# First attention of a two-layer kernel: the transposed maxima move from the maxima's banks to the scores' banks

## The reference

```
qkv = zn @ w_qkv                      # 16 heads of 8
scores = einsum('bhqd,bhkd->bhqk', q, k) / SCALING
att = softmax(scores, axis=-1)
out = einsum('bhal,bhlv->bhav', att, v)
out = out @ w_proj + b_proj
```

## Time and profile before

| | |
|---|---|
| profiled execution: span | 1372.0 us |
| median of three runs | 1371.8 us |
| TensorE matmul busy | 1249.1 us, 91% |
| VectorE busy | 1009.4 us, 74% |
| ScalarE busy | 851.8 us, 62% |
| GpSimd busy | 237.5 us, 17% |
| first attention, first to last exponential | 116.6 to about 811 us |

### The profile page before, as it was taken

How to read it: one execution, slowest core, us unless ns; L and a number is a source line. 1 busy time by engine, 2 the same in 40 slices (tenths; PEclk the granted TensorE clock), 3 DMA queues, 4 the chain that set the end, 5 groups by cost and what they waited for, 6 DMA issues and landing times. The chain is left out here.

```text
span 1372.0 us, 25967 instructions
## 1 busy us (share of the span) xinstructions
PE 1249.1 (91%) x10305; PEld 580.1 (42%) x10305; DVE 1009.4 (74%) x1288; ACT 851.8 (62%) x1447; POOL 237.5 (17%) x309
## 2 busy tenths in 40 slices
PE   6968999999999999999999978998899899899980
PEld 4631222222222222222222225555699566688870
DVE  6878898998899989998999737665676588623324
ACT  3533888888888888888888866555421366533431
POOL 4200110000000000000000002000385222135560
PEclk9986999999999999999999989998999599999995
DMA  5763033232323313222231121100011111123316
GB/s 147 202 199 79 26 65 64 50 76 45 74 64 82 76 40 78 51 66 66 50 74 40 69 71 48 47 16 16 17 31 39 55 44 36 46 69 102 100 58 188
DMA packets 75204, 94.96 MB, mean 69 GB/s; under 512 B 13236, under 2 KB 44684, under 8 KB 74052
## 3 DMA queue, kind: packets, MB, share of 16 engines
q1 hardware_dynamic: 69996, 83.19, 23.9%
q0 software_dynamic: 5088, 10.12, 2.4%
HBM read 54.30 MB, written 38.56 MB: 68 GB/s over the span
## 5 line engine op out<-in xcount | busy, mean ns | idle before, releaser
L670 ACT ACTIVATE b_exp_ring<-psum 128x512 f32<-128x512 f32 x1024 | 555.6, 600 | 148.8 <-PE psum L725 145.6
L612 DVE TENSOR_REDUCE b_mx<-psum 128x2 f32<-128x1024 f32 x507 | 595.8, 1218 | 66.5 <-PE psum L557 65.4
L725 PE MATMUL psum<-b_q,b_k 75*128 75x512 bf16 x1024 | 312.4, 387 | 1.5 <-ACT b_exp_ring L670 1.5
L701 PE MATMUL psum<-b_exp_ring,b_v 128*32 128x512 f32 x2048 | 274.5, 608 | 0.9 <-ACT b_exp_ring L670 0.7
L725 PEld LDWEIGHTS psum<-b_q,b_k 75*128 75x128 bf16 x1024 | 79.3, 97 | 317.0 <-ACT b_exp_ring L670 221.8
L556 PE MATMUL psum<-b_k,b_q 64*128 64x512 bf16 x512 | 168.9, 395 | 25.5 <-DVE b_mx L612 10.6
L557 PE MATMUL psum<-b_ko,b_qo 64*128 64x512 bf16 x512 | 168.9, 395 | 0.0
L740 POOL CAST b_neg<-b_neg_rest 16x128 bf16<-16x128 f32 x32 | 8.9, 279 | 639.6 <-DVE b_neg_rest L623 639.6
L1834 ACT ACTIVATE e_hT<-psum,e_b 128x358 f32<-128x358 f32 (+3 forms) x96 | 53.6, 559 | 75.4 <-PE psum L1854 72.0
L556 PEld LDWEIGHTS psum<-b_k,b_q 64*128 64x128 bf16 x512 | 44.7, 93 | 128.6 <-DVE b_mx L612 41.4
L701 PEld LDWEIGHTS psum<-b_exp_ring,b_v 128*32 128x32 f32 x2048 | 41.3, 108 | 108.6 <-issue 106.0
(11 more groups left out here) (278 smaller groups left out, 1427.6 us busy)
## 6 DMA issues: line engine op xcount, KB each, us to landing
b_q<-q_ops SPq DMA_DIRECT2D x48, 192.0 KB
b_k<-k_ops SPq DMA_DIRECT2D x48, 192.0 KB
k_ops<-a_k SPq DMA_DIRECT2D x20, 256.0 KB, 3.3
x_disp<-b_zeros SPq DMA_DIRECT2D x13, 320.0 KB
e_x<-x_disp SPq DMA_DIRECT2D x8, 520.0 KB
v_ops<-a_vs SPq DMA_DIRECT2D x4, 1024.0 KB, 5.1
b_v<-v_ops SPq DMA_DIRECT2D x16, 256.0 KB
av_out<-b_acc SPq DMA_DIRECT2D x128, 32.0 KB, 1.7
```

Source lines behind the costliest of these rows:

```text
L612: nc.vector.reduce_max(mx[:, d % 2, :, i // 2, i % 2], pair, AX.X).then_inc(sem("b_max_done"), 1)
L670: act.activation(ex[:, n % E_RING, :], g.bank(5 + n % 3), ACT.Exp, scale=ATT_SCALE)\
L701: last = nc.tensor.matmul(AV[32 * i:32 * i + 32, :], v[s][:, at_v:at_v + 32], ex[:, (4 * group + i) % E_RING, :], start=(kb == 0), stop=(k ...
L725: nc.tensor.matmul(g.bank(5 + n % 3), k[s][0:XROWS, h, kb * P:(kb + 1) * P], q[s][0:XROWS, h, half * BANK:(half + 1) * BANK], start=True, ...
```

## The change

- `max_items` goes; the maxima's sequence holds the 512 items alone, two behind each group, `MAX_LEAD` = 10 past the first item of the duo after.
- The sequence of the score banks gets the transposed maxima as units of their own (`score_units`): `(0, None)` first, and `(d+1, None)` ahead of the tiles of group `T_GROUP` = 4 of duo d. TensorE transposes into the next of banks 5 to 7; ScalarE copies the 16x128 negated to a new tile `b_neg_all`; GpSimd casts the first part, subtracts, casts the second and subtracts again. SyncE stores each part when it is there.
- VectorE folds the halves of duo d (`both_halves`) after the reduction of the first item of duo d+1.
- VectorE's reciprocals stand behind an item number; the multiplication for `d_oT` stands behind the last item.

```diff
-ITEMS = MAXES + 1
-LATE = 2
-T_GROUP = 5
-LEAD = ITEMS + LATE - 2 * T_GROUP
+NMAX = DUOS * MAXES
+MAX_LEAD = 10
+T_GROUP = 4
...
+def score_units():
+
+    seq = [(0, None)]
     for d in range(DUOS):
+        for kb in range(TB):
+            if kb == T_GROUP and d + 1 < DUOS:
+                seq.append((d + 1, None))
+            seq += [(d, 4 * kb + i) for i in range(4)]
+    return seq
...
+    units = score_units()
+    place = {unit: n for n, unit in enumerate(units)}
+    issued = lambda d, kb: min(NMAX, MAXES * (d + 1) + 2 * kb + MAX_LEAD)
...
+            def both_halves(d):
+                dve.wait_ge(sem("b_max_done"), MAXES * (d + 1))
+                nc.vector.reduce_max(m[:, d % 2, :], mx[:, d % 2, :, :, :].rearrange("p h t a -> p (h t) a"),
+                                     AX.X).then_inc(sem("b_m"), 1)
+
+            for n in range(FIRST, NMAX):
                 item(n)
+                if n >= MAXES and n % MAXES == 0:
+                    both_halves(n // MAXES - 1)
+                d = n // MAXES - 1
                 b = d // 8 - 1
+                if 0 <= b < RECS and d % 8 == 3 and n % MAXES == 8:
                     dve.wait_ge(sem("d_dens"), 16 * (b + 1))
                     nc.vector.reciprocal(dens[:, b, :], dens[:, b, :]).then_inc(sem("d_recs"), 1)
+            both_halves(DUOS - 1)
+            for b in range(EARLY):
+                dve.wait_ge(sem("d_loaded"), 32 * (b + 1))
+                nc.vector.tensor_tensor(oT[:, b, :], num[:, :], den[:, :], ALU.mult).then_inc(sem("d_oT"), 1)
...
+            def negated_maxima(d, bank):
+                if d:
+                    act.wait_ge(sem("b_third"), d)
+                act.activation(neg_all[:, :], bank[0:MAXES, 0:P], ACT.Copy, scale=-1.0).then_inc(sem("b_exp_done"), 1)
...
+            def bank_of(n):
+                if n >= 3:
+                    pe.wait_ge(sem("b_exp_done"), n - 2)
+                return g.bank(5 + n % 3)
+
+            def transposed_maxima(d):
+                pe.wait_ge(sem("b_m"), d + 1)
+                to = bank_of(place[d, None])
+                nc.tensor.transpose(to[0:MAXES, 0:P], m[:, d % 2, :], g.ident[:, :]).then_inc(sem("b_scores"), 1)
...
+            for n in range(FIRST, MAXES + 2):
+                item(n)
+            transposed_maxima(0)
+            for n in range(MAXES + 2, issued(0, 0)):
                 item(n)
             for d in range(DUOS):
                 pe.wait_ge(sem("b_m_loaded"), 16 * NPART * (d + 1))
                 for kb in range(TB):
                     if d == DUOS - 1 and kb in PROJECT_AT:
                         project_piece(PROJECT_AT.index(kb))
+                    n = issued(d, kb)
+                    if kb == T_GROUP and d + 1 < DUOS:
+                        transposed_maxima(d + 1)
+                    scores(d, 4 * kb)
+                    scores(d, 4 * kb + 1)
+                    scores(d, 4 * kb + 2)
+                    if d + kb:
+                        times_v(TB * d + kb - 1)
+                    scores(d, 4 * kb + 3)
+                    for i in range(n, min(n + 2, NMAX)):
+                        item(i)
...
             def parts(d):
-                pool.wait_ge(sem("b_max_done"), seq.index((d, None)) + 1)
+                pool.wait_ge(sem("b_exp_done"), place[d, None] + 1)
+                if d:
+                    pool.wait_ge(sem("b_m_loaded"), 16 * NPART * d)
+                nc.gpsimd.tensor_copy(neg[:, 0, :], neg_all[:, :]).then_inc(sem("b_first"), 1)
+                pool.wait_ge(sem("b_first"), d + 1)
+                nc.gpsimd.tensor_tensor(neg_rest[:, :], neg_all[:, :], neg[:, 0, :], ALU.subtract)\
+                  .then_inc(sem("b_rest"), 1)
+                pool.wait_ge(sem("b_rest"), d + 1)
                 nc.gpsimd.tensor_copy(neg[:, 1, :], neg_rest[:, :]).then_inc(sem("b_second"), 1)
...
-                    if i == 0:
-                        sp.wait_ge(sem("b_max_done"), seq.index((d, None)) + 1)
-                    else:
-                        sp.wait_ge(sem(("b_second", "b_third")[i - 1]), d + 1)
+                    sp.wait_ge(sem(("b_first", "b_second", "b_third")[i]), d + 1)
```

More of the change, by code:

```diff
@@ L557, in maxima_scores @@
     return g.nc.tensor.matmul(g.bank(2 * (n % 2) + 1), qo[MROWS:P, p, t], ko[MROWS:P, p, keys], start=True, stop=True)
-def max_items():
-    seq = []
+def score_units():
+    seq = [(0, None)]
     for d in range(DUOS):
[L564 to L568, removed]
+        for kb in range(TB):
[3 more added lines that the diff above has]
+    return seq
 def layer0_attention(g):
@@ L583, in layer0_attention @@
         m = sb("b_m", [P, 2, MAXES])
+        neg_all = sb("b_neg_all", [MAXES, P])
         neg_rest = sb("b_neg_rest", [MAXES, P])
@@ L598, in layer0_attention @@
     AV = g.bank(4)
-    seq = max_items()
-    through = lambda kb: 2 * (kb + 1) + (kb >= T_GROUP)
-    upto = lambda d, kb: min(len(seq), ITEMS * (d + 1) - 1 + LEAD + through(kb))
+    units = score_units()
+    place = {unit: n for n, unit in enumerate(units)}
+    issued = lambda d, kb: min(NMAX, MAXES * (d + 1) + 2 * kb + MAX_LEAD)
     with nc.Block() as block:
@@ L607, in item @@
             def item(n):
-                d, i = seq[n]
+                d, i = n // MAXES, n % MAXES
                 dve.wait_ge(sem("b_max_scores"), n + 1)
[L610 to L626, removed]
+                pair = g.bank(2 * (n % 2), 2).rearrange("p (h x) -> p h x", h=2)
@@ L627, in _ @@
+                nc.vector.reduce_max(mx[:, d % 2, :, i // 2, i % 2], pair, AX.X).then_inc(sem("b_max_done"), 1)
+            def both_halves(d):
[3 more added lines that the diff above has]
+            for n in range(FIRST, NMAX):
                 item(n)
-            for d in range(DUOS):
-                for n in range(upto(d, -1), upto(d, TB - 1)):
-                    item(n)
+                if n >= MAXES and n % MAXES == 0:
+                    both_halves(n // MAXES - 1)
+                d = n // MAXES - 1
@@ L631, in _ @@
                 b = d // 8 - 1
-                if 0 <= b < RECS and d % 8 == 3:
+                if 0 <= b < RECS and d % 8 == 3 and n % MAXES == 8:
                     dve.wait_ge(sem("d_dens"), 16 * (b + 1))
                     nc.vector.reciprocal(dens[:, b, :], dens[:, b, :]).then_inc(sem("d_recs"), 1)
-                if 0 <= b < EARLY and d % 8 == 7:
-                    dve.wait_ge(sem("d_loaded"), 32 * (b + 1))
-                    nc.vector.tensor_tensor(oT[:, b, :], num[:, :], den[:, :], ALU.mult).then_inc(sem("d_oT"), 1)
+            both_halves(DUOS - 1)
@@ L662, in evacuate @@
                 act.activation(acc[:, d % 2, :], AV, ACT.Copy).then_inc(sem("b_acc"), 1)
[L664 to L673, removed]
+            def negated_maxima(d, bank):
+                if d:
+                    act.wait_ge(sem("b_third"), d)
+                act.activation(neg_all[:, :], bank[0:MAXES, 0:P], ACT.Copy, scale=-1.0).then_inc(sem("b_exp_done"), 1)
+            for n, (d, u) in enumerate(units):
+                act.wait_ge(sem("b_scores"), n + 1)
+                if u is None:
+                    negated_maxima(d, g.bank(5 + n % 3))
+                    continue
+                e = 4 * TB * d + u
+                if e >= E_RING:
+                    act.wait_ge(sem("b_av"), (e - E_RING) // 4 + 1)
+                act.activation(ex[:, e % E_RING, :], g.bank(5 + n % 3), ACT.Exp, scale=ATT_SCALE)\
+                   .then_inc(sem("b_exp_done"), 1)
+                if u == 3 and d:
+                    evacuate(d - 1)
             evacuate(DUOS - 1)
@@ L684, in item, with scores @@
                     pe.wait_ge(sem("b_max_done"), n - 1)
[L685 to L689, removed]
-                maxima_scores(g, q[s], k[s], qo[s], ko[s], n, p, i).then_inc(sem("b_max_scores"), 1)
+                maxima_scores(g, q[s], k[s], qo[s], ko[s], n, p, i).then_inc(sem("b_max_scores"), 1)
+            def bank_of(n):
[6 more added lines that the diff above has]
+                nc.tensor.transpose(to[0:MAXES, 0:P], m[:, d % 2, :], g.ident[:, :]).then_inc(sem("b_scores"), 1)
+            def scores(d, u):
+                s, h, kb, half = d // 2 % SLOTS, 2 * (d % 2) + u % 4 // 2, u // 4, u % 2
+                nc.tensor.matmul(bank_of(place[d, u]), k[s][0:XROWS, h, kb * P:(kb + 1) * P],
+                                 q[s][0:XROWS, h, half * BANK:(half + 1) * BANK], start=True, stop=True)\
+                  .then_inc(sem("b_scores"), 1)
             def times_v(group):
@@ L695, in times_v @@
                 s, p = d // 2 % SLOTS, d % 2
-                pe.wait_ge(sem("b_exp_done"), 4 * (group + 1))
+                pe.wait_ge(sem("b_exp_done"), place[d, 4 * kb + 3] + 1)
                 if kb == 0 and d:
@@ L706, in project_piece @@
                 if piece == 0:
-                    pe.wait_ge(sem("b_max_done"), len(seq))
+                    pe.wait_ge(sem("b_max_done"), NMAX)
                     pe.wait_ge(sem("d_oT"), 1)
@@ L712, in _ @@
```

(6 more changed lines are left out.)

## The result

The changed kernel takes 1399.9 us (median of four runs, 1396.0 to 1406.2) against 1371.6 before. The ratio is 1.021, 95% interval 1.018 to 1.025: slower, by 28 us. The forecast was 1401 within 1392 to 1410. The profiled execution is the fastest of the four: span 1394.3 us, against 1372.0 before.

A forecast was written before the change was run, and what follows sets the result against it. It took TensorE (98.3% busy) to bound the middle of the first attention, VectorE close behind. Terms 47.7 - 19.5 + 1.5 - 0.7 - 0.2 = +28.8 us on a span of 1372.0 gave 1400.8, forecast 1401, range 1392 to 1410.

The forecast's parts named there:

- The wait for the fold: Transposition ahead of group 4 waits for VectorE's fold, queued behind a just-issued item's reduction: +1.59 us a duo, +47.7 us.
- What is removed: The longer group with the old transposed maxima goes (3.26 us against 2.61): 0.65 us a duo, -19.5 us over 30 duos.
- the ring: Three score banks: the third score tile behind the transposition waits 0.11 us a duo for ScalarE's copy.
- The net of a duo: Per duo (eight groups of four score tiles): +1.59 us of wait less 0.65 removed; duos of 22.6 us, not 21.64.
- The clock: Rival: each stall in the first attention lowers TensorE's clock, 4 us lost each, 120 in all, 1521 us; chance 0.03.
- The reciprocals: VectorE's three reciprocals in the first attention stay; no cost was counted for them.
- The start: Before the first scores: 26 items instead of 24, +2.26 us, less a 0.79 interruption; together +1.5 us.
- oT: Its multiplication moves behind the last maximum, where VectorE is idle: -0.7 us.
- The last transposition: The stage's last transposition waits less for its fold: -0.2 us, bounds -0.5 and +0.3.
- the chain of parts: GpSimd's parts and their stores: 6.0 us at worst after the transposition, 10.4 available; hidden, 4 us to spare.
- The 0.05 of signalling: Added to the transposition-to-copy time and ScalarE's copy, 0.32 + 0.28 + 0.05 = 0.65 us, before the third score tile starts.
- The rule on TensorE's order: Matmuls stay in program order, so ready scores cannot pass the waiting transposition; otherwise the first rival's 1360 us, chance 0.06.

The follow-up runs named there:

- taken away in two ways: Changed kernel with VectorE's fold ahead of the first item's reduction: 1357.7 us; or changed kernel with the transposed maxima one group later (T_GROUP = 5): 1361.1 us.
- the fold first: Changed kernel with VectorE folding duo d+1's halves ahead of the reduction of duo d+2's first item, not behind it: 1357.7 us, ratio 0.990.
- a lead of 4: Kernel with the fold ahead of the reduction, plus MAX_LEAD = 4, transposed maxima in group 7, reciprocals behind the second item: 1424.8 us, ratio 1.041.

## Why the prediction was right, step by step

The stage by itself, from its first matmul to the end of its last copy out of bank 4, took 718.9 us before (94.36 to 813.29) and 746.3 after (95.17 to 841.50): +27.4. The stages behind took 558.7 and 552.8 in the two profiled executions, although nothing was changed in them; their stretches at the lower clock lie elsewhere (between 1060 and 1100 us at 0.57 to 0.58 before; after, 0.72 and 0.68 between 1080 and 1120), and in the other profiled kernels they took 555.1 to 557.2. This is why the profiled span is 6 us under the forecast while the median is 1 us from it. Single runs lie between 1396.0 and 1406.2 us, so that last agreement, to 1 us, is closer than the terms deserve.

- **The wait for the fold** was the mechanism, at its place and in its size. Forecast 1.91 us from item to transposition, measured 1.81; forecast 4.20 from item to item, measured 4.08; +1.47 a duo in place of +1.59. The term that was off is from the fold's start to the transposition: 0.34 us was read in the one place of the earlier trace rows, and 0.24 it is (313.36 to 313.60; in the changed kernel's last duo 0.25, 809.82 to 810.07). Why the kernel before has 0.1 more there stays open. That the wait is the cause is shown from three sides: taken away in two ways the kernel is 39 to 42 us faster, lengthened by one reduction the duo is 1.12 us longer.
- **What is removed.** A duo without the stall is 21.19 us against 21.64: -0.45. With 0.20 for the transposition and the ring in it, what went is 0.65, as forecast; the seven other groups take 21.19 - 2.81 = 18.38 us, as before (21.64 - 3.26). Nothing came of VectorE's two operations fewer, as assumed.
- **The net of a duo**: 22.46 - 21.64 = +0.82, against 1.59 - 0.65 = 0.94; thirty make +24.6 instead of +28.2.
- **The clock** was no term of the sum, and as a rival (a fall each time, 4 us each) it was wrong both ways: it falls after some of the stalls, 2 and 6 of 30, and a fall costs 1.53 us. +3.1 to +9.2 us. The row before 1196.32 showed that a gap of 1.41 us may leave the clock alone, and I took "may" for "does". By luck this about makes up for the smaller stall, which left the net 3.6 us under the forecast.
- **The reciprocals** were written down as unchanged. They stand now between the two items of a group and not between groups: 0.77 us a duo and not 0.39, three times, +1.1. A step that is moved has to be priced at its new place.
- **The start.** First scores 22.9 us after the stage's first matmul and not 21.6: +1.3, forecast +1.5. But most of it was given back. The clock rose just before 128 us before and just after 126 us in the changed kernel (granted 0.53 and 0.93 in the stretch from 126 to 128), so the later start spent less time at 1.2 GHz: duo 0's result left bank 4 28.6 us after the first scores before, and 27.7 after, with a stall of 0.8 in it.
- **oT** behind the last item: its duo is 22.46 us like the others, -0.7 as forecast.
- **The last transposition** waited 0.37 us for its fold and not 0.48: 0.1 of the 0.2 us forecast is seen.
- **ScalarE and GpSimd**: 0.09 us of ring a duo (forecast 0.11), and the chain of parts hidden. The 0.05 of signalling stood on no row of before; in the changed kernel the copy ends at 314.18 and the weight load of the third score tile, which waited for it, starts at 314.23.

In the stage: 24.6 + 3.1 + 1.1 + 1.3 - 0.7 = 29.4, less about 1.7 for duo 0's shorter slow part (28.6 - 27.7, and the stall of 0.8 in it) is 27.7; measured 27.4, where the forecast had 28.8.

The rule on TensorE's order held: the scores of group 4 never passed the waiting transposition. Of the rule that idle gaps between bursts put the clock back (the Trainium skill, "TensorE: Matmul & The Clock Gate", Why this matters for your kernels) this case shows that gaps shorter than those the page warns of count too: stalls of 1.20 us in dense work did it in 2 and in 6 of 30 cases, stalls of 2.33 us in 9 of 30.

## What to carry to other kernels

Where an in-order engine waits for a small result, read from the consumer's place what was *issued last to the producer* ahead of that result; one reduction too many there, issued just before the wait, cost this kernel 1.2 us thirty times, and moving one line turned 2.1% slower into 1.0% faster. Price an instruction that is moved at its new place even if it is the same instruction. A short stall in an otherwise dense stage can cost more than its length, because the clock may fall after it; look for such falls in the granted clock by stretches and in the length of the single duos, not in the spread of the runs, which doesn't tell here.

The best kernels here, with the fold first, the transposed maxima in group 5 or 6 with a lead of 8 or 6, and the reciprocals between groups, take 1352.6 and 1352.0 us: 1.2 to 1.3% under the kernel before, and 47 us under the changed one. Between these two there is no difference that was measured.

## What was not expected of the hardware

The clock's falls. After stalls of 1.20 us it fell in 2, then in 6 of 30 duos of the same kernel, at other places each time, and cost 1.53 us. After stalls of 2.33 us it fell in 9 of 30 and cost 3.0 to 4.4 us. In the kernel with a lead of 4 it never fell after the first fourteen waits of 1.21 to 1.40 us, and then after ten of the next sixteen, which were 1.25 to 3.08 us long. What decides in a single case stays open. At the start of the stage the clock rose at about 121 to 128 us whether the scores began at 113 or at 118 us, so an earlier start brought everything or nothing: with a lead of 8 in place of 10 the first scores came 2.2 us earlier and duo 0's result 3.1, and with 6 in place of 8 they came 2.3 us earlier and the result no earlier at all.
